# Cross attention on one Trainium2 core: six fold pairs in one piece ahead of the last batch's mixing, against two pieces of two inside it

## The chip, the core and the metric

The kernel runs on one core of one Trainium2 chip. The core has five engines with a queue each: TensorE (PE), VectorE (DVE), ScalarE (ACT), GpSimd (POOL) and SyncE (SP), which here issues most of the transfers. They meet only through semaphores. The metric is the device time of one execution in microseconds; lower is better.

## The reference, cut to what matters

The block is a Perceiver layer over 64 batches of 32 tokens of width 512, with 257 context rows each: cross attention, a small attention over heads, and a gated MLP. The change touches the cross attention alone:

```
xn = layernorm(x, ln_gamma, ln_beta)
q = (xn @ w_q).reshape(B, SQ, 16, 64)
k, v = split(context @ w_kv)            # 257 rows per batch
scores = einsum('bqhd,bkhd->bhqk', q * SCALE, k)
attn = softmax(scores)
out = einsum('bhqk,bkhd->bqhd', attn, v).reshape(B, SQ, 1024)
out = out @ w_out + b_out
```

The kernel never forms k or v. It folds the weight into the query, q·(w_k for that head), which gives a vector of width 512 for each head and token, takes scores of that against the raw context, mixes the raw context with the probabilities, and multiplies the mix by w_v.

## The kernel before

**Tiling.** `cross_attention` works in 16 turns (`TURNS`) of 4 batches (`GB`): 15 iterations of a hardware loop, `turn(t, True)`, and a last `turn(15, False)`. A turn has 128 tokens. Values that must keep their precision are kept as a high and a low part, and a product is three matmuls (`three`, L82 to L84).

**Folding.** `fold_pair(t, 1, j)` (L540) makes the folded queries of heads 2j and 2j+1 of the *next* turn: 8 matmuls, each of which is two records in the profile. A head has 64 elements, so its matmuls contract 64 rows, and two of them run side by side in the two halves of the array. Each pair fills two PSUM banks, one for each head. `FOLD_BANK` gives pairs 0, 3 the banks `A`, pairs 1, 4, 7 the banks `B2`, and pairs 2, 5, 6 the banks `C`, which are the banks that the transposed probabilities (`T_BANK`) use too. ScalarE copies each bank to a rounded high part (`high_fold`, L780), VectorE then subtracts that from the bank to get the low part (`low_fold`, L686), and raises `fold_lo`. `FOLD_AFTER` says how many of these low parts must be done before a later pair may overwrite the banks:

```
FOLD_BANK = (A, B2, C, A, B2, C, C, B2)
FOLD_AFTER = {3: 2, 4: 4, 5: 6, 6: 12, 7: 10}
```

So pair 3 waits for both low parts of pair 0, pair 4 for those of pair 1, pair 5 for those of pair 2.

**Mixing.** `mix_chunk(t, b, c)` makes a quarter of batch b's mix with six 512-column matmuls in bank 6 or 7, in turn. Before it starts it waits until the chunk two before it has been copied out by VectorE's `keep_mix` (L679): chunk 2 of batch 3 waits for `keep_mix(t, 3, 0)`, chunk 3 for `keep_mix(t, 3, 1)`. Chunk 0 also waits for the low parts of the batch's transposed probabilities (`pT_lo`). Between `keep_mix(t, 3, 0)` and the next copy VectorE has `keep_last` (a transpose, L691, a wait for it, and a multiplication, L694).

**Output.** `out_half(t, 0)` (L600 and L607) multiplies the mix by w_v; its products of chunk 3 wait for `keep_mix(t, 3, 3)`. Then come fold pairs 6 and 7, the first scores of the next turn and `out_half(t, 1)`.

**Order.** Every engine's order is written out by hand in its own `turn`. ScalarE's queue has the twelve high parts of pairs 0 to 5 in a row, and it is not edited.

Of the kernel before, what the change touches and what calls it, by code (L numbers as in the profile page):

```python
# [74 lines left out]
def f32(ap):  # L75

    return ap.bitcast(F32)
# [245 lines left out]
def cross_attention(nc, hw, ahead, ctx_nat, ctx_T, last_T, q_dram, v_dram, o_hi, o_lo, identity, heads):  # L323
# [9 lines left out]
    GB = P // SQ  # L333
    TURNS = B // GB
    KT = SK // P
# [5 lines left out]
    with ExitStack() as ctx:  # L341
# [34 lines left out]
        pT_hi, pT_lo = s.count("pT_hi", GB * KT), s.count("pT_lo", GB * KT)  # L376
# [20 lines left out]
        def of_head(a, h):  # L397

            return a[:, :, :, h * SQ:(h + 1) * SQ].rearrange("p c b n -> p (c b) n")
# [131 lines left out]
        def _(pe):  # L531
            def fold_pair(t, ahead, j):
                if j == 0:
                    pe.wait_ge(q_loaded.sem, q_loaded.at(t, 16 * (ahead + 1)))
                if j in FOLD_AFTER:
                    pe.wait_ge(fold_lo.sem, fold_lo.at(t, 2 * PAIRS * ahead + FOLD_AFTER[j]))
                for c in range(DC):
                    for h in range(2):
                        r = slice(h * HE, (h + 1) * HE)
                        mm = pe.matmul(ps[:, FOLD_BANK[j][h], c * P:(c + 1) * P], wk[r, j, c * P:(c + 1) * P],  # L540
                                       q[r, j, :], start=True, stop=True)
                mm.then_inc(fold_ready.sem, 1)
# [21 lines left out]
            def scores(t, b):  # L564
                pe.wait_ge(Tlo_done.sem, Tlo_done.at(t, b + 1))
                for i in range(TILES):
                    pe.wait_ge(exp_done.sem, exp_done.at(t, (b - 1) * TILES + i + 1))
                    score_tile(b, i)

            def turn_probs(t, b):  # L570
                for i in range(TILES):
                    pe.wait_ge(probs_ready.sem, probs_ready.at(t, b * TILES + i + 1))
                    for k in range(KT):
                        mm = pe.transpose(ps[:, T_BANK[k], i * P:(i + 1) * P], prob[:, i, k * P:(k + 1) * P], ident[:, :])
                        if i == TILES - 1:
                            mm.then_inc(turned.sem, 1)
# [34 lines left out]
            def turn(t, more):  # L611
                for b in range(GB - 1):
                    turn_probs(t, b)
                    scores(t, b + 1)
                    if b < GB - 2:
                        for c in range(DC):
                            mix_chunk(t, b, c)
                mix_chunk(t, 2, 0)
                mix_chunk(t, 2, 1)
                turn_probs(t, 3)  # L620
                mix_chunk(t, 2, 2)
                mix_chunk(t, 2, 3)
                if more:
                    fold_pair(t, 1, 0)
                    fold_pair(t, 1, 1)
                for c in range(DC):
                    mix_chunk(t, 3, c)
                    if more and c % 2 == 0:
                        fold_pair(t, 1, 2 + c)
                        fold_pair(t, 1, 3 + c)  # L630
                out_half(t, 0)
                if more:
                    fold_pair(t, 1, 6)
                    fold_pair(t, 1, 7)
                    for i in range(TILES):
                        first_scores(t, 1, i)
                out_half(t, 1)
# [15 lines left out]
        @block.vector  # L653
        def _(dve):
            def row_max(t, b, i):
                dve.wait_ge(scores_ready.sem, scores_ready.at(t, b * TILES + i + 1))
                dve.tensor_reduce(negmax[:, i:i + 1], ps[:, S_BANK[i], 0:SK], AX_X, ALU.max, negate=True)\  # L657
                    .then_inc(max_done.sem, 1)

            def invert(t, b, i):  # L660
                dve.wait_ge(exp_done.sem, exp_done.at(t, b * TILES + i + 1))
                dve.reciprocal(share[:, i:i + 1], total[:, i:i + 1]).then_inc(share_done.sem, 1)  # L662

            def softmax(t, b):
                for i in range(TILES):
                    row_max(t, b, i)
                    if i > 0:
                        invert(t, b, i - 1)
                invert(t, b, TILES - 1)

            def split_probs(t, b):
                for k in range(KT):
                    dve.wait_ge(pT_hi.sem, pT_hi.at(t, b * KT + k + 1))
                    dve.tensor_tensor(pT[b % 2][1][:, k, :], ps[:, T_BANK[k], :], f32(pT[b % 2][0][:, k, :]), ALU.subtract)\
                        .then_inc(pT_lo.sem, 1)

            def keep_mix(t, b, c):
                dve.wait_ge(mixed.sem, mixed.at(t, b * DC + c + 1))
                dve.tensor_copy(mix[:, c, b, :], ps[:, M_BANK[c % 2], :]).then_inc(mix_kept.sem, 1)  # L679

            def low_fold(t, ahead, j):
                for h in range(2):
                    n = 2 * j + h
                    dve.wait_ge(fold_hi.sem, fold_hi.at(t, 2 * PAIRS * ahead + n + 1))
                    hi, lo = (of_head(a, n) for a in fold)
                    dve.tensor_tensor(lo, ps[:, FOLD_BANK[j][h], :].rearrange("p (c n) -> p c n", n=SQ), f32(hi),  # L686
                                      ALU.subtract).then_inc(fold_lo.sem, 1)

            def keep_last(t):
                dve.wait_ge(last_ready.sem, last_ready.at(t, GB))  # L690
                dve.transpose(last_t[:, :, :], last_z[:, :, :]).then_inc(last_turned.sem, 1)  # L691
                dve.wait_ge(last_turned.sem, last_turned.at(t, 1))
                dve.wait_ge(o_ready.sem, o_ready.at(t, 0))
                dve.tensor_tensor(last_p[:, :, :, :],  # L694
                                  last_t[:, :, :].rearrange("p i (b q) -> p i b q", b=1).to_broadcast([P, TILES, GB, SQ]),
                                  own[:, :].rearrange("p (i b q) -> p i b q", i=1, q=1).to_broadcast([P, TILES, GB, SQ]),
                                  ALU.mult).then_inc(last_kept.sem, 1)

            def low_out(t, m):
                dve.wait_ge(o_hi_done.sem, o_hi_done.at(t, m + 1))  # L700
                dve.tensor_tensor(o[1][:, :, :], ps[:, O_BANK[m], :].rearrange("p (j n) -> p j n", n=P),
                                  f32(o[0][:, :, :]), ALU.subtract).then_inc(o_lo_done.sem, 1)

            def turn(t, more):
                for b in range(GB - 1):
                    split_probs(t, b)
                    softmax(t, b + 1)
                    if b < GB - 2:
                        for c in range(DC):
                            keep_mix(t, b, c)  # L710
                keep_mix(t, 2, 0)
                keep_mix(t, 2, 1)
                split_probs(t, 3)
                keep_mix(t, 2, 2)
                if more:
                    low_fold(t, 1, 0)
                keep_mix(t, 2, 3)
                if more:
                    low_fold(t, 1, 1)
                for c in range(DC):  # L720
                    keep_mix(t, 3, c)
                    if c == 0:
                        keep_last(t)
                    if more and c > 0:
                        low_fold(t, 1, 1 + c)
                    elif not more:
                        w_low(dve, range(2 * c + 1, 2 * c + 3, 2))
                if more:
                    low_fold(t, 1, 5)
                low_out(t, 0)  # L730
                if more:
                    low_fold(t, 1, 6)
                    low_fold(t, 1, 7)
                    softmax(t, GB)
                else:
                    w_low(dve, range(9, 15, 2))
                low_out(t, 1)
                if not more:
                    w_low(dve, range(15, PIECES, 2))

            dve.sem_inc(o_lo_done.sem, 2)
            dve.wait_ge(once, 16 + 16 * HT)
            for j in range(PAIRS):
                low_fold(0, 0, j)
            softmax(0, 0)
            dve.wait_ge(v_stored, 16)
            with dve.Fori(0, TURNS - 1) as t:
                turn(t, True)
            turn(TURNS - 1, False)

        @block.scalar
# [902 lines left out]
```

## Time and profile before

| | |
|---|---|
| median of 3 executions | 1916.24 us (1915.59 to 1916.68) |
| profiled execution | 1916.39 us, of which the span from first to last instruction is 1914.6 us |
| TensorE busy in the span | 1857.1 us (97%) |
| VectorE, ScalarE, GpSimd busy | 1039.1, 666.2 and 558.6 us |
| turn of the loop (islands of the same kind, 389.27 to 456.07) | 66.80 us |

A busy share is of the whole span. A matmul's row begins before the one ahead of it has ended, since the engine pipelines them; so the distance from start to start says what one costs. Times in the timeline views are from the start of the span. The idle time in brackets behind a row is that of the engine just before it, with what ended it. A row that stands for many instructions (x32) gives the start of the first and the time from there to the end of the last.

### The profile page before, as it was taken

How to read it: one execution, taken by the hardware profiler on the slowest of the kernel's cores; microseconds unless marked ns; L12 is line 12 of the kernel's file. 1: busy time of each engine (PE TensorE's matmuls, PEld its weight loads, DVE VectorE, ACT ScalarE, POOL GpSimd, SP SyncE). 2: the span in 40 equal slices, each digit the busy share in tenths (PEclk: the TensorE clock that was granted, in tenths of full speed). 3: DMA queues.
4: the chain of work that ended last, by engine and by line, in shares of the span. 5: the costliest groups of instructions: out<-in, count | busy, mean ns of one | idle time of the engine just before them, and what ended most of it. 6: DMA issues, size and time to landing. Idle time of an engine off the chain costs nothing. (4 is left out here: it accounts for less than half of the span.)

```text
span 1914.6 us, 36622 instructions
## 1 busy us (share of the span) xinstructions
PE 1857.1 (97%) x14096; PEld 1607.2 (84%) x14096; DVE 1039.1 (54%) x2015; ACT 666.2 (35%) x1356; POOL 558.6 (29%) x546
## 2 busy tenths in 40 slices
PE   5989999999999999999999999599999999999999
PEld 4868988988998898899989888488888788888887
DVE  7614555455455545545554555388889763333322
ACT  3235444444444444444444445221111231111111
POOL 3015334433533444353344436231112000000000
PEclk9999999999999999999999999799999999999999
DMA  7323223322322332232233223633352131000000
GB/s 244 128 85 99 86 61 103 99 77 77 110 78 66 99 99 78 76 110 77 67 98 99 81 73 127 184 84 88 99 154 73 57 126 65 3 34 32 21 24 22
DMA packets 166629, 165.65 MB, mean 87 GB/s; under 512 B 8688, under 2 KB 123888, under 8 KB 166576
## 3 DMA queue, kind: packets, MB, share of 16 engines
q1 hardware_dynamic: 162144, 156.27, 27.1%
q10 hardware_dynamic: 4432, 8.65, 1.2%
q8 instruction: 36, 0.59, 0.1%
q14 instruction: 17, 0.14, 0.0%
HBM read 131.08 MB, written 33.82 MB: 86 GB/s over the span
## 5 line engine op out<-in xcount | busy, mean ns | idle before, releaser
L497 POOL TENSOR_TENSOR x_prob<-x_prob,x_share 128x256 f32<-128x256 f32 x256 | 157.0, 613 | 602.9 <-DVE x_share L662 595.7
L82 PE MATMUL x_ps<-w_cT_hi,w_space_hi 128*128 128x258 f32 x1024 | 296.1, 289 | 0.0
L83 PE MATMUL x_ps<-w_cT_lo,w_space_hi 128*128 128x258 f32 x1024 | 290.7, 284 | 0.0
L84 PE MATMUL x_ps<-w_cT_hi,w_space_lo 128*128 128x258 f32 x1024 | 288.5, 282 | 0.0
L679 DVE COPY x_mix<-x_ps 128x512 f32<-128x512 f32 x256 | 176.2, 688 | 115.1 <-PE x_ps L84 114.9
L82 PE MATMUL x_ps<-x_pT_hi,x_cn_hi 128*128 128x512 f32 x512 | 208.1, 406 | 1.5 <-DVE x_mix L679 1.5
L686 DVE TENSOR_TENSOR w_space_lo<-x_ps,w_space_hi 128x512 fp32r<-128x512 f32 x256 | 161.0, 680 | 78.4 <-ACT w_space_hi L780 45.8
L84 PE MATMUL x_ps<-x_pT_hi,x_cn_lo 128*128 128x512 f32 x512 | 201.2, 393 | 0.0
L769 ACT ACTIVATE x_prob<-x_ps,x_negmax 128x257 f32<-128x257 f32 x256 | 122.1, 477 | 227.1 <-DVE x_negmax L657 227.1
L83 PE MATMUL x_ps<-x_pT_lo,x_cn_hi 128*128 128x512 f32 x512 | 199.7, 390 | 0.0
L657 DVE TENSOR_REDUCE x_negmax<-x_ps 128x1 f32<-128x257 f32 x256 | 108.1, 422 | 166.2 <-PE x_ps L84 166.2
L82 PEld LDWEIGHTS x_ps<-w_cT_hi,w_space_hi 128*128 128x128 f32 x1024 | 193.8, 189 | 2.0 <-issue 0.2
L83 PEld LDWEIGHTS x_ps<-w_cT_lo,w_space_hi 128*128 128x128 f32 x1024 | 193.8, 189 | 0.0
L84 PEld LDWEIGHTS x_ps<-w_cT_hi,w_space_lo 128*128 128x128 f32 x1024 | 193.5, 189 | 0.0
L780 ACT ACTIVATE w_space_hi<-x_ps 128x512 fp32r<-128x512 f32 x256 | 132.4, 604 | 124.0 <-PE x_ps L540 124.0
L491 POOL TENSOR_TENSOR x_cn_lo<-e_raw_n,x_cn_hi 128x1024 fp32r<-128x1024 f32 x64 | 153.3, 2395 | 0.0
L540 PEld LDWEIGHTS x_ps<-e_q,e_wk 64*128 64x128 f32 x2048 | 122.2, 192 | 27.7 <-issue 18.7
L486 POOL TENSOR_TENSOR w_cT_lo<-e_raw_T,w_cT_hi 128x1028 fp32r<-128x1028 f32 x64 | 141.5, 2210 | 5.8 <-ACT w_cT_hi L757 5.8
L540 PE MATMUL x_ps<-e_q,e_wk 64*128 64x128 f32 x2048 | 134.4, 282 | 7.5 <-SPq L465 4.9
L600 PE MATMUL x_ps<-x_mix,e_wv 128*64 128x128 f32 x2048 | 138.3, 275 | 0.8 <-DVE x_mix L679 0.8
L600 PEld LDWEIGHTS x_ps<-x_mix,e_wv 128*64 128x64 f32 x2048 | 114.2, 137 | 12.3 <-issue 5.4
L82 PEld LDWEIGHTS x_ps<-x_pT_hi,x_cn_hi 128*128 128x128 f32 x512 | 96.1, 188 | 23.6 <-DVE x_mix L679 1.9
(205 smaller groups left out, 3546.6 us busy)
## 6 DMA issues: line engine op xcount, KB each, us to landing
e_raw_T<-ctx_T SPq DMA_DIRECT2D x64, 514.0 KB, 4.0
e_raw_n<-ctx_nat SPq DMA_DIRECT2D x64, 512.0 KB, 3.6
q<-q_q ACTq DMA_DIRECT2D x16, 512.0 KB, 2.8
e_q<-q SPq DMA_DIRECT2D x16, 512.0 KB, 4.2
o_hi<-x_o_hi SPq DMA_DIRECT2D x32, 256.0 KB, 2.4
o_lo<-x_o_lo SPq DMA_DIRECT2D x32, 256.0 KB, 3.0
a_oT_hi<-o_hi SPq DMA_DIRECT2D x16, 512.0 KB, 4.4
a_oT_lo<-o_lo SPq DMA_DIRECT2D x16, 512.0 KB, 5.6
```

The source lines that it names most:

```text
L82: pe.matmul(out, lhs[0], rhs[0], start=start, stop=False)
L83: pe.matmul(out, lhs[0], rhs[1], start=False, stop=False)
L84: return pe.matmul(out, lhs[1], rhs[0], start=False, stop=stop)
L486: pool.tensor_tensor(cT[b % 2][1][:, :, 0:SK], raw_T[:, :, :], f32(cT[b % 2][0][:, :, 0:SK]), ALU.subtract).then_inc(Tlo_done.sem, 1)
L491: pool.tensor_tensor(cn[b % 2][1][:, :, :], raw_n[:, :, :], f32(cn[b % 2][0][:, :, :]), ALU.subtract).then_inc(nlo_done.sem, 1)
L497: pool.tensor_tensor(prob[:, i, 0:KT * P], prob[:, i, 0:KT * P], share[:, i:i + 1].to_broadcast([P, KT * P]), ALU.mult)\
L540: mm = pe.matmul(ps[:, FOLD_BANK[j][h], c * P:(c + 1) * P], wk[r, j, c * P:(c + 1) * P], q[r, j, :], start=True, stop=True)
L600: pe.matmul(out[h], w_v[:, c, n * HE:(n + 1) * HE], mix[:, c, :, n * SQ:(n + 1) * SQ], start=c == 0, stop=False)
L679: dve.tensor_copy(mix[:, c, b, :], ps[:, M_BANK[c % 2], :]).then_inc(mix_kept.sem, 1)
L686: dve.tensor_tensor(lo, ps[:, FOLD_BANK[j][h], :].rearrange("p (c n) -> p c n", n=SQ), f32(hi), ALU.subtract).then_inc(fold_lo.sem, 1)
L769: act.activation(prob[:, i, 0:SK], ps[:, S_BANK[i], 0:SK], ACT.Exp, bias=negmax[:, i:i + 1], accum_out=total[:, i:i + 1]).then_inc(exp_don ...
L780: act.activation(of_head(fold[0], 2 * j + h), ps[:, FOLD_BANK[j][h], :].rearrange("p (c n) -> p c n", n=SQ), ACT.Copy)\
```

## The change

On TensorE pairs 2, 3, 4 and 5 move from behind chunks 0 and 2 of batch 3's mixing to a place ahead of chunk 0, straight behind pairs 0 and 1. The wait for `pT_lo` that chunk 0 made is made ahead of pair 2, since its banks are those of the transposed probabilities. On VectorE all twelve low parts of pairs 0 to 5 stand in a row behind `keep_mix(t, 2, 3)`, ahead of the four copies of batch 3. The last turn, which folds nothing, keeps its order.

```
@@ tensor: turn
                 if more:
                     fold_pair(t, 1, 0)
                     fold_pair(t, 1, 1)
+                    pe.wait_ge(pT_lo.sem, pT_lo.at(t, GB * KT))
+                    for j in range(2, 6):
+                        fold_pair(t, 1, j)
                 for c in range(DC):
                     mix_chunk(t, 3, c)
-                    if more and c % 2 == 0:
-                        fold_pair(t, 1, 2 + c)
-                        fold_pair(t, 1, 3 + c)
                 out_half(t, 0)
@@ vector: turn
                 keep_mix(t, 2, 2)
-                if more:
-                    low_fold(t, 1, 0)
                 keep_mix(t, 2, 3)
                 if more:
-                    low_fold(t, 1, 1)
+                    for j in range(6):
+                        low_fold(t, 1, j)
                 for c in range(DC):
                     keep_mix(t, 3, c)
                     if c == 0:
                         keep_last(t)
-                    if more and c > 0:
-                        low_fold(t, 1, 1 + c)
-                    elif not more:
+                    if not more:
                         w_low(dve, range(2 * c + 1, 2 * c + 3, 2))
-                if more:
-                    low_fold(t, 1, 5)
                 low_out(t, 0)
```

TensorE's queue of before, from the last matmul of batch 2's mixing on. `e_q,e_wk` are the folds (x16 is two pairs), `x_pT,x_cn` the mixing, and a REGISTER_ALU row computes the value of a wait that stands there:

```order
L84 MATMUL x_ps<-x_pT_hi,x_cn_lo 128x512
L534 REGISTER_ALU
L540 MATMUL x_ps<-e_q,e_wk 128x128 x16
L587 REGISTER_ALU
L82 MATMUL x_ps<-x_pT_hi,x_cn_hi 128x512
L83 MATMUL x_ps<-x_pT_lo,x_cn_hi 128x512
L84 MATMUL x_ps<-x_pT_hi,x_cn_lo 128x512
L587 REGISTER_ALU
L82 MATMUL x_ps<-x_pT_hi,x_cn_hi 128x512
L83 MATMUL x_ps<-x_pT_lo,x_cn_hi 128x512
L84 MATMUL x_ps<-x_pT_hi,x_cn_lo 128x512
L540 MATMUL x_ps<-e_q,e_wk 128x128 x8
```

The same place of TensorE's queue in the changed kernel, up to the first matmul of chunk 0:

```order
L540 MATMUL x_ps<-e_q,e_wk 128x128 x16
L626 REGISTER_ALU
L540 MATMUL x_ps<-e_q,e_wk 128x128 x8
L536 REGISTER_ALU
L540 MATMUL x_ps<-e_q,e_wk 128x128 x8
L536 REGISTER_ALU
L540 MATMUL x_ps<-e_q,e_wk 128x128 x8
L536 REGISTER_ALU
L540 MATMUL x_ps<-e_q,e_wk 128x128 x8
L587 REGISTER_ALU
L82 MATMUL x_ps<-x_pT_hi,x_cn_hi 128x512
```

The six matmuls of chunk 0 that stood between pairs 1 and 2, and chunks 1 and 2 that stood between pairs 3 and 4, are behind all six pairs now; the waits on `fold_lo` (L536) of pairs 3, 4 and 5 have nothing but folds ahead of them.

VectorE's queue of before, from the copy of batch 2's chunk 2 on (`w_space_lo` is a low part of a fold, `x_mix` a copy of a mixing chunk):

```order
L679 COPY x_mix<-x_ps 128x512
L684 REGISTER_ALU
L686 TENSOR_TENSOR w_space_lo<-x_ps,w_space_hi 128x16x32
L684 REGISTER_ALU
L686 TENSOR_TENSOR w_space_lo<-x_ps,w_space_hi 128x16x32
L679 COPY x_mix<-x_ps 128x512
L684 REGISTER_ALU
L686 TENSOR_TENSOR w_space_lo<-x_ps,w_space_hi 128x16x32
L684 REGISTER_ALU
L686 TENSOR_TENSOR w_space_lo<-x_ps,w_space_hi 128x16x32
L679 COPY x_mix<-x_ps 128x512
L690 ISA
```

VectorE's queue of the changed kernel, from the last two of the twelve low parts on:

```order
L686 TENSOR_TENSOR w_space_lo<-x_ps,w_space_hi 128x16x32
L684 REGISTER_ALU
L686 TENSOR_TENSOR w_space_lo<-x_ps,w_space_hi 128x16x32
L679 COPY x_mix<-x_ps 128x512
L690 ISA
L691 STREAM_TRANSPOSE x_last_t<-x_last_z 128x128
L692 REGISTER_ALU
L693 ISA
L694 TENSOR_TENSOR x_last_p<-x_last_t,x_own 128x512
L679 COPY x_mix<-x_ps 128x512 x3
```

The copy of batch 3's chunk 0, which had four low parts ahead of it, has twelve ahead of it now, and the other three copies follow `keep_last` with nothing between them.

## Rows read from the trace of the kernel before

**Rows 1.** The page: busy time by engine, and the granted TensorE clock by slice

```profile
PE 1857.1 (97%) x14096; PEld 1607.2 (84%) x14096; DVE 1039.1 (54%) x2015; ACT 666.2 (35%) x1356; POOL 558.6 (29%) x546
PEclk9999999999999999999999999799999999999999
```

**Rows 2.** Busy time by stretch: wake of a long wait, the stage, a turn

```profile
core 0: us, PE busy (x) PEld busy (x) DVE busy (x) ACT busy (x) POOL busy (x), PEclk, DMA share, GB/s
140.00:144.00 4.00, 3.69 (x33) 3.47 (x34) 1.46 (x3) 1.21 (x3) 0.00 (x0) 0.58 0.02 4
389.27:401.37 12.10, 12.10 (x121) 9.86 (x120) 8.26 (x14) 6.20 (x12) 0.32 (x1) 1.00 0.25 81
389.27:456.07 66.80, 66.80 (x609) 60.28 (x608) 35.80 (x76) 30.48 (x66) 28.60 (x29) 1.00 0.29 87
```

**Rows 3.** The waits of TensorE between 200 and 1210 us

```profile
PE x_ps L82 <- DVE x_mix L679: 1.5, 1, 1.5
PE x_ps L600 <- DVE x_mix L679: 0.8, 1, 0.8
```

**Rows 4.** Timeline of TensorE around pairs 0 and 1 (start, duration, instruction)

```profile
388.95 0.40 PE L84 MATMUL x_ps<-x_pT_hi,x_cn_lo 128*128 128x512 f32 x1
389.27 2.06 PE L540 MATMUL x_ps<-e_q,e_wk 64*128 64x128 f32 x32
391.26 0.50 PE L82 MATMUL x_ps<-x_pT_hi,x_cn_hi 128*128 128x512 f32 x1
391.60 0.39 PE L83 MATMUL x_ps<-x_pT_lo,x_cn_hi 128*128 128x512 f32 x1
391.83 0.40 PE L84 MATMUL x_ps<-x_pT_hi,x_cn_lo 128*128 128x512 f32 x1
```

**Rows 5.** Timeline of TensorE, window 134.6 to 135.1: a fold's first six records

```profile
134.74 0.60 PE L540 MATMUL x_ps<-e_q,e_wk 64*128 64x128 f32 x6
```

**Rows 6.** Timeline of VectorE, same turn as rows 4

```profile
387.13 1.29 DVE L674 TENSOR_TENSOR x_pT_lo<-x_ps,x_pT_hi 128x512 fp32r<-128x512 f32 x2 [0.70 <-ACT x_pT_hi L775]
391.11 1.29 DVE L686 TENSOR_TENSOR w_space_lo<-x_ps,w_space_hi 128x512 fp32r<-128x512 f32 x2 [2.09 <-ACT w_space_hi L780]
...
394.11 0.68 DVE L679 COPY x_mix<-x_ps 128x512 f32<-128x512 f32 x1
394.71 0.30 DVE L691 STREAM_TRANSPOSE x_last_t<-x_last_z 128x128 f32<-128x128 f32 x1
395.14 0.69 DVE L694 TENSOR_TENSOR x_last_p<-x_last_t,x_own 128x512 f32<-128x512 f32 x1
...
401.48 0.69 DVE L679 COPY x_mix<-x_ps 128x512 f32<-128x512 f32 x1 [1.27 <-PE x_ps L84]
```

**Rows 7.** Timeline of ScalarE, same turn: high parts of pairs 0 and 1

```profile
390.48 2.07 ACT L780 ACTIVATE w_space_hi<-x_ps 128x512 fp32r<-128x512 f32 x4 [2.89 <-PE x_ps L540]
```

**Rows 8.** Timeline of VectorE in the kernel's opening folds: six low parts in a row

```profile
136.58 3.68 DVE L686 TENSOR_TENSOR w_space_lo<-x_ps,w_space_hi 128x512 fp32r<-128x512 f32 x6 [2.24 <-ACT w_space_hi L780]
```

**Rows 9.** Timeline of TensorE in the opening folds: pairs 3 to 5, then 6 and 7

```profile
134.74 2.95 PE L540 MATMUL x_ps<-e_q,e_wk 64*128 64x128 f32 x48
140.31 3.52 PE L540 MATMUL x_ps<-e_q,e_wk 64*128 64x128 f32 x32 [2.62 <-DVE w_space_lo L686]
```

**Rows 10.** Timeline of VectorE in the last turn, around a copy that comes late

```profile
1194.06 0.88 DVE L694 TENSOR_TENSOR x_last_p<-x_last_t,x_own 128x512 f32<-128x512 f32 x1
1194.86 1.78 DVE L394 TENSOR_TENSOR w_cT_lo<-e_wk,w_cT_hi 128x512 fp32r<-128x512 f32 x1
1196.56 0.68 DVE L679 COPY x_mix<-x_ps 128x512 f32<-128x512 f32 x1
```

**Rows 11.** Timeline of TensorE at the same place

```profile
1195.43 0.39 PE L84 MATMUL x_ps<-x_pT_hi,x_cn_lo 128*128 128x512 f32 x1
1197.29 0.50 PE L82 MATMUL x_ps<-x_pT_hi,x_cn_hi 128*128 128x512 f32 x1 [1.47 <-DVE x_mix L679]
1197.64 0.39 PE L83 MATMUL x_ps<-x_pT_lo,x_cn_hi 128*128 128x512 f32 x1
```

**Rows 12.** Timeline of TensorE where the mixing ends and the output begins

```profile
401.05 0.39 PE L84 MATMUL x_ps<-x_pT_hi,x_cn_lo 128*128 128x512 f32 x1
401.37 1.29 PE L600 MATMUL x_ps<-x_mix,e_wv 128*64 128x128 f32 x16
```

## The prediction

> **What bounds the kernel now.** I read the page first. TensorE is busy for 97% of the span, at the full clock nearly throughout [rows 1]. Then the windows view: one turn of the loop takes 66.80 us and TensorE is busy in all of it, at full clock [rows 2]. Then TensorE's waits: between 200 and 1210 us there are two, of 1.5 and 0.8 us, both on a VectorE copy of the mix and both in the last turn, which folds nothing [rows 3]. So in the 15 turns of the loop no engine holds TensorE up in a way that this view counts, and the time of a turn is the time of TensorE's own queue. What the change can give must be a cheaper queue on TensorE. What it can cost is any new wait there. I then read TensorE, VectorE and ScalarE over one turn, the one whose pair 0 starts at 389.27. Other turns differ by hundredths.
>
> **What is removed: two changes of form.** Before, TensorE goes from full-height matmuls to half-height folds and back three times in this stretch; after, once. The price is in [rows 4]. From the last mixing matmul, 388.95, to the second one behind the folds, 391.60, pass 2.65 us. Of that 0.23 is the normal step of a mixing matmul (391.60 to 391.83), twice: 0.46. The folds run two by two, 16 steps for two pairs. What does one step cost? A record of a fold lasts 0.27 (two records that start together after the first), so the x32 row's last pair of records starts 2.06 − 0.27 = 1.79 behind its first, 15 steps, and in [rows 5] the third starts 0.60 − 0.27 = 0.33 behind, 2 steps. With a first step a and later ones b: a + b = 0.33, a + 14b = 1.79, so b = 0.112 and a = 0.215. Sixteen plain steps are 1.79 us. The rest, 2.65 − 0.46 − 1.79 = 0.40 us, is the price of going in and out once. Two are removed: **−0.80 us a turn**. The Trainium skill, TensorEngine Tiling, Key Properties, says that changing the tiling mode drains TensorE; by that rule alone the change is a gain, and the trace agrees with the drain. The same page's section PSUM Bottleneck says the contrary for this change: tiling speeds up TensorE but not the emptying of PSUM, which may become the bottleneck. Rows decide between the two as follows.
>
> **What is added: waits on VectorE's drain.** A pair costs TensorE 8 × 0.112 = 0.90 us. It costs VectorE two low parts. Their pace is in [rows 8]: six in a row take 3.68, and the last lasts 0.68, so they start 0.60 apart, 1.20 us for each pair. ScalarE's high parts start (2.07 − 0.60)/3 = 0.49 apart [rows 7], 0.98 for each pair. VectorE is the slowest of the three and sets the rhythm. Mixing stood between the folds before and gave it the time; now it doesn't.
>
> Now the turn step by step. TensorE starts pair 0 at 389.27, and without a wait would start pair 3 at 389.27 + 0.10 + 3 × 0.90 = 392.07. VectorE starts the first low part at 391.11 [rows 6]; nothing ahead of it is in its way then, since it has idled for 2.09 us, and the copy of batch 2's chunk 3, which now stands ahead, can start at about 389.4, when that matmul ends, and takes 0.68. The low parts of pair j then start at 391.11 + 1.20j and 0.60 later, and the second ends 0.68 after that. How soon does TensorE go on? In [rows 8, 9] VectorE ends at 140.26 and TensorE starts at 140.31; in [rows 10, 11] at 1197.24 and 1197.29: 0.05. And a restarted engine pays a first step that is longer: 0.10 for folds (0.215 against 0.112), and 0.11 for mixing (1197.29 to 1197.64 is 0.35, normal 0.23).
>
> - Pair 3 waits for pair 0: released at 391.11 + 0.60 + 0.68 + 0.05 = 392.44, late by 0.37, restart 0.10.
> - Pair 4 is ready at 392.44 + 1.00 = 393.44, released at 393.64: 0.20, restart 0.10.
> - Pair 5 is ready at 394.64, released at 394.84: 0.20, restart 0.10.
> - Chunk 0 of batch 3 starts at 394.84 + 1.00 + 0.10 = 395.94. It needs no late copy; chunk 1 starts 0.11 + 6 × 0.23 = 1.49 later, at 397.43, and chunk 2 would at 398.81.
> - VectorE's thirteenth instruction of the row is the copy of chunk 0: it starts at 391.11 + 12 × 0.60 = 398.31 and ends at 398.99. Chunk 2 starts at 399.04: late by 0.23, restart 0.11.
> - Behind that copy comes `keep_last`: its transpose 0.60 later, its multiplication 0.43 after the transpose [rows 6], the next copy 0.61 after that (an instruction starts 0.08 before the end of the one ahead; 1194.06 + 0.88 against 1194.86 in [rows 10]). The copy of chunk 1 starts at 398.31 + 0.60 + 0.43 + 0.61 = 399.95 and ends at 400.63. Chunk 3, ready at 399.04 + 1.49 = 400.53, starts at 400.68: 0.15, restart 0.11.
> - Its last matmul starts 0.11 + 5 × 0.23 = 1.26 later at 401.94, and the output 0.32 behind that (401.05 to 401.37 in [rows 12]) at 402.26. Before, it started at 401.37.
>
> That is **+0.89 us a turn**. Summed the other way: waits 0.37 + 0.20 + 0.20 + 0.23 + 0.15 = 1.15, restarts 3 × 0.10 + 2 × 0.11 = 0.52, less 0.80: 0.87. I take 0.88. What matters is that the end of this stretch is one chain on VectorE from 391.11 to 400.63, with little left to TensorE: as long as VectorE is fed, the waits at pairs 3 to 5 don't add to it.
>
> Is it fed? ScalarE begins a pair's high parts about when the fold ends, and the first low part can start when the first high part is done, 1.84 us after the start of a pair in [rows 4, 6] (389.27 to 391.11). For pair 3: 392.44 + 1.84 = 394.28 against VectorE's 394.71; pair 4: 395.48 against 395.91; pair 5: 396.68 against 397.11. Slack 0.43 at each, so yes.
>
> The other edits cost nothing. The wait for `pT_lo` ahead of pair 2 is met: VectorE ended that work at 387.13 + 1.29 = 388.42 [rows 6], and pair 2 starts at 391.17. Uncovered, it would stop TensorE until that end. The copy of chunk 3 before the output is a wait now as before: VectorE has idled 1.27 us when it starts at 401.48, just behind the last mixing matmul [rows 6, 12], and after the change it is again idle then, having only copies left. VectorE is free 2.4 us sooner behind that, but pairs 6 and 7, the first scores and the high parts of the output wait for TensorE or ScalarE, so nothing comes back. ScalarE's and GpSimd's queues and the transfers keep their order and move with TensorE.
>
> **The sum.** 15 turns × 0.88 = 13.2 us on the profiled execution's 1916.39 gives 1929.6. The median of the runs shown is 0.15 lower: I say **1929.4 us**, 0.7% slower.
>
> **Bounds.** VectorE's pace enters about 13 times; at 0.01 either way it is 0.13 us a turn, 2 us in all. The release of 0.05 and the restart at 0.10 come in at the last wait once each; the nearest rows for them span 0.05 to 0.11. A restart inside folds at full clock is not in the trace, but it drops out of the VectorE chain. So 1927 to 1932 for this case alone.
>
> **The rivals.** About 0.2% (3.8 us) is what a measurement of this kernel can tell from no change.
>
> *The drain keeps up (faster).* TensorE would go through six pairs with no wait, and only the two changes of form would count: 15 × −0.80 = −12 us, 1904. This is where the rule on the drain of TensorE alone would lead. It decides at a VectorE pace of 0.45 us for each low part (half of a pair's 0.90), with the first release at or before 392.07. [Rows 8] show 0.60 with ScalarE working beside it, and [rows 6] the first release 0.37 too late even then. Chance 6%, with everything between it and no change.
>
> *The debt stays in the folds.* If VectorE caught up before chunk 2 (its copies jumping in somewhere, or faster than their rows), only 0.77 + 0.30 − 0.80 = +0.27 us a turn remains: +4, 1920. Against it: 12 × 0.60 is simple counting, and [rows 10, 11] show a late copy stopping TensorE just here, by 1.47 us in the last turn. Chance 6%, of which some 4% fall within 0.2%.
>
> *The clock falls (far slower).* In the opening folds, TensorE waited 2.62 us, and the next two pairs took 3.52 us where they take 2.06 at full clock [rows 4, 9]; the granted clock there was 0.58, a mix of full speed and half of it, 1.2 GHz [rows 2]. Were each turn to lose it for a stretch like that, it would add about 1.5 us: 15 × (0.88 + 1.5) = 36, 1952. Against it: the longest single wait that I find is 0.37 us, and the wait of 1.47 us in [rows 11] was followed by normal steps of 0.23 to 0.35. It decides at a wait between 1.47 and 2.62 us. Chance 3%.
>
> **How the numbers follow.** The forecast case has 85%. Together: faster 0.05, same 0.05, slower 0.90. The range for 8 in 10 is the forecast's own, widened a little for a term that I have missed by 0.15 to 0.3 us a turn: 1925 to 1933; it leaves the three rivals out, 15% in all.
>
> **What would show it.** In the timeline of a turn: one TensorE row of folds broken by waits on `w_space_lo` of 0.2 to 0.4 us less what the profile's overlap hides (a record outlives its step by 0.16, so waits of 0.20 may hardly be listed as idle); TensorE waits on `x_mix` ahead of chunks 2 and 3; twelve low parts as one unbroken VectorE row of about 7.3 us (11 × 0.60 + 0.68) without idle time, then the copy, and a distance of 12.99 us from pair 0 to the output where it was 12.10. The loop's turn grows to 67.68 us. I am wrong if VectorE's row has gaps (ScalarE then sets the pace), if it runs faster than 0.60, or if the granted clock drops inside the loop.

## The result, and the profile after

| | before | after |
|---|---|---|
| median | 1916.46 us (1915.59 to 1919.39, 4 runs) | 1930.70 us (1930.66 to 1931.03, 4 runs) |
| ratio | | 1.0072, 95% interval 1.0055 to 1.0089 |
| span of the profiled execution | 1914.6 us | 1928.9 us |

The change makes the kernel 14.2 us slower. 1929.4 us was forecast.

The page has TensorE busy for the same share as in [rows 1]. The granted clock by slice differs in the third slice alone, which ends ahead of the loop:

```profile
span 1928.9 us, 36622 instructions
PE 1866.5 (97%) x14096; PEld 1609.5 (83%) x14096; DVE 1040.8 (54%) x2015; ACT 667.7 (35%) x1356; POOL 559.0 (29%) x546
PEclk9989999999999999999999999799999999999999
```

The busy time of TensorE has grown by 9.4 us with the same number of instructions. That isn't more work: a record that overlaps its neighbour less counts for more.

The windows view, for the stage from pair 0 to the output and for one turn (columns as in [rows 2]; the turn chosen is again the fourth):

```profile
392.47:405.46 12.99, 12.62 (x121) 9.94 (x121) 10.76 (x18) 6.31 (x12) 0.33 (x1) 1.00 0.24 75
392.47:460.22 67.75, 67.38 (x609) 60.43 (x609) 35.91 (x76) 30.58 (x66) 28.64 (x29) 1.00 0.29 86
```

The stage takes 12.99 us where [rows 2] had 12.10. TensorE's matmuls are idle for only 0.37 us of it by this view, and the clock is full. The fourth turn takes 67.75 us where 67.68 was forecast. Turns differ by up to 0.11 us here, and by 0.08 before, so one turn is a rough measure: from pair 0 of the first turn to that of the fifteenth the mean is 67.70 us, against 66.85 before.

TensorE's timeline at the folds, and behind it at chunks 1 to 3 of the mixing and the output:

```profile
392.15 0.40 PE L84 MATMUL x_ps<-x_pT_hi,x_cn_lo 128*128 128x512 f32 x1
392.47 2.95 PE L540 MATMUL x_ps<-e_q,e_wk 64*128 64x128 f32 x48
395.66 3.55 PE L540 MATMUL x_ps<-e_q,e_wk 64*128 64x128 f32 x48 [0.23 <-DVE w_space_lo L686]
399.14 0.50 PE L82 MATMUL x_ps<-x_pT_hi,x_cn_hi 128*128 128x512 f32 x1
...
401.77 0.39 PE L84 MATMUL x_ps<-x_pT_hi,x_cn_lo 128*128 128x512 f32 x1
402.23 0.51 PE L82 MATMUL x_ps<-x_pT_hi,x_cn_hi 128*128 128x512 f32 x1
...
403.50 0.40 PE L84 MATMUL x_ps<-x_pT_hi,x_cn_lo 128*128 128x512 f32 x1
403.87 0.50 PE L82 MATMUL x_ps<-x_pT_hi,x_cn_hi 128*128 128x512 f32 x1
...
405.46 0.55 PE L600 MATMUL x_ps<-x_mix,e_wv 128*64 128x128 f32 x6
```

Both rows of folds hold three pairs. The first takes 2.95 us, the second 3.55: the 0.60 us more are the waits and restarts of pairs 4 and 5, which no idle figure of these rows names. Only the wait ahead of pair 3 is listed, as 0.23 us; from the starts it is 395.66 − 392.47 − 0.10 − 24 × 0.112 = 0.40, and 0.37 was forecast. At chunks 2 and 3 the distance from the matmul ahead is 0.46 and 0.37 where 0.23 is normal, and again nothing stands in brackets. Waits shorter than a record's overlap have to be read from start-to-start distances, or from the weight loads, which the profile lists as an engine of their own (PEld). A weight load's record is shorter, and each of the five waits stands in brackets there:

```profile
395.65 0.97 PEld L540 LDWEIGHTS x_ps<-e_q,e_wk 64*128 64x128 f32 x16 [0.42 <-DVE w_space_lo L686]
396.85 0.97 PEld L540 LDWEIGHTS x_ps<-e_q,e_wk 64*128 64x128 f32 x16 [0.23 <-DVE w_space_lo L686]
398.04 0.97 PEld L540 LDWEIGHTS x_ps<-e_q,e_wk 64*128 64x128 f32 x16 [0.22 <-DVE w_space_lo L686]
...
402.23 0.19 PEld L82 LDWEIGHTS x_ps<-x_pT_hi,x_cn_hi 128*128 128x128 f32 x1 [0.50 <-DVE x_mix L679]
...
403.87 0.19 PEld L82 LDWEIGHTS x_ps<-x_pT_hi,x_cn_hi 128*128 128x128 f32 x1 [0.41 <-DVE x_mix L679]
```

VectorE's timeline over the same stage, with ScalarE's twelve high parts as the last row (line numbers move with an edit: the high parts are L780 before and L775 here):

```profile
392.58 0.69 DVE L679 COPY x_mix<-x_ps 128x512 f32<-128x512 f32 x1 [0.36 <-PE x_ps L84]
394.31 7.26 DVE L686 TENSOR_TENSOR w_space_lo<-x_ps,w_space_hi 128x512 fp32r<-128x512 f32 x12 [1.04 <-ACT w_space_hi L775]
401.50 0.68 DVE L679 COPY x_mix<-x_ps 128x512 f32<-128x512 f32 x1
402.10 0.30 DVE L691 STREAM_TRANSPOSE x_last_t<-x_last_z 128x128 f32<-128x128 f32 x1
402.53 0.69 DVE L694 TENSOR_TENSOR x_last_p<-x_last_t,x_own 128x512 f32<-128x512 f32 x1
403.14 1.49 DVE L679 COPY x_mix<-x_ps 128x512 f32<-128x512 f32 x2
405.57 0.69 DVE L679 COPY x_mix<-x_ps 128x512 f32<-128x512 f32 x1 [0.94 <-PE x_ps L84]
...
393.68 6.66 ACT L775 ACTIVATE w_space_hi<-x_ps 128x512 fp32r<-128x512 f32 x12 [2.89 <-PE x_ps L540]
```

From 394.31 to the copy of chunk 1 VectorE has no gap but the 0.13 us in which `keep_last` waits for its own transpose. The copy of chunk 0 ends at 401.50 + 0.68 = 402.18 and chunk 2 starts at 402.23; the copy of chunk 1 ends 0.05 ahead of chunk 3 likewise. The last row, the copy of chunk 3, ends 13.79 us behind pair 0; in [rows 4, 6] it ended 12.90 us behind.

TensorE's waits between 200 and 1210 us, against [rows 3], where the loop had none (the two of the last turn come later than 1210 now):

```profile
PE x_ps L540 <- DVE w_space_lo L686: 3.3, 14, 0.2
```

The same view of the weight loads has two on VectorE at L540 and L82 that the loop of before didn't have:

```profile
PEld x_ps L82 <- DVE x_mix L679: 13.0, 29, 0.5
PEld x_ps L540 <- DVE w_space_lo L686: 12.2, 42, 0.4
```

That is 25.2 us in 14 turns. The forecast's waits and restarts, before the 0.80 that the change saves, are 1.67 us a turn, 23.4 in 14 turns.

### The profile page after: what moved, and what is told of

The parts are those of the page before. It is cut to its first block and busy times, and to the rows that moved or that the text cites. A ratio compares the mean times of both kernels' runs of the same rounds, so it can differ in the third digit from the quotient of the medians.

```text
span 1928.9 us, 36622 instructions
## 1 busy us (share of the span) xinstructions
PE 1866.5 (97%) x14096; PEld 1609.5 (83%) x14096; DVE 1040.8 (54%) x2015; ACT 667.7 (35%) x1356; POOL 559.0 (29%) x546
## 5 line engine op out<-in xcount | busy, mean ns | idle before, releaser
L82 PE MATMUL x_ps<-w_cT_hi,w_space_hi 128*128 128x258 f32 x1024 | 296.1, 289 | 0.0
L82 PE MATMUL x_ps<-x_pT_hi,x_cn_hi 128*128 128x512 f32 x512 | 207.9, 406 | 2.4 <-DVE x_mix L679 1.5
L82 PEld LDWEIGHTS x_ps<-w_cT_hi,w_space_hi 128*128 128x128 f32 x1024 | 193.7, 189 | 2.0 <-issue 0.2
L686 DVE TENSOR_TENSOR w_space_lo<-x_ps,w_space_hi 128x512 fp32r<-128x512 f32 x256 | 156.3, 682 | 62.9 <-DMA x_own<-identity 32.4
L775 ACT ACTIVATE w_space_hi<-x_ps 128x512 fp32r<-128x512 f32 x256 | 134.0, 604 | 64.1 <-PE x_ps L540 58.7
L540 PE MATMUL x_ps<-e_q,e_wk 64*128 64x128 f32 x2048 | 138.7, 284 | 12.0 <-DVE w_space_lo L686 6.1
L540 PEld LDWEIGHTS x_ps<-e_q,e_wk 64*128 64x128 f32 x2048 | 123.6, 192 | 30.1 <-DVE w_space_lo L686 16.8
L82 PEld LDWEIGHTS x_ps<-x_pT_hi,x_cn_hi 128*128 128x128 f32 x512 | 96.1, 188 | 33.5 <-DVE x_mix L679 15.4
```

Of the source, the lines that this page charges most:

```text
L82: pe.matmul(out, lhs[0], rhs[0], start=start, stop=False)
L775: act.activation(of_head(fold[0], 2 * j + h), ps[:, FOLD_BANK[j][h], :].rearrange("p (c n) -> p c n", n=SQ), ACT.Copy)\
```

## The experiments

For each run I read one distance in its trace, in the fourth turn of the loop: from the start of pair 0 to the end of the copy of chunk 3 of batch 3. The output needs that copy before it can go on. Before: 12.90; after: 13.79. The mean turn is that of the 14 turns from the first pair 0 of the loop to the fifteenth, against 66.85 us before.

| run | pair 0 to output | pair 0 to end of last copy | against before, a turn | mean turn against before | ratio to before (95%) |
|---|---|---|---|---|---|
| after | 12.99 | 13.79 | +0.89 | +0.85 | 1.0072 (1.0055 to 1.0089) |
| e_last_later | 12.72 | 13.52 | +0.62 | +0.59 | 1.0051 (1.0034 to 1.0068) |
| e_copies_first | 12.53 | 13.17 | +0.27 | +0.25 | 1.0017 (1.0008 to 1.0027) |
| e_copies_all | 12.38 | 13.18 | +0.28 | +0.23 | 1.0021 (1.0012 to 1.0031) |
| e_four_pieces | 12.52 | 13.32 | +0.42 | +0.39 | 1.0029 (1.0020 to 1.0039) |
| e_two_of_three | 11.68 | 12.48 | −0.42 | −0.44 | 0.9953 (0.9937 to 0.9970) |
| e_half_after | 11.59 | 12.39 | −0.51 | −0.53 | 0.9971 (0.9959 to 0.9983) |
| e_half_before | 12.10 | 12.90 | 0.00 | −0.02 | 0.9999 (0.9990 to 1.0009) |

e_last_later, e_copies_first, e_four_pieces and e_two_of_three ran on one chip, where the kernel before had 1918.06 us (19 runs), e_copies_all and the two with halved low parts on another, where it had 1917.15 (22 runs). The expectations name totals that start from 1916.5, so a total is to be judged against the kernel before on its own chip, as the ratio does. For every run, fifteen times the fourth column lies within the interval of the ratio.

**Copies ahead of the last low parts (e_copies_first).** VectorE's order alone is changed, from the changed kernel:

```
                 if more:
-                    for j in range(6):
+                    for j in range(5):
                         low_fold(t, 1, j)
                 for c in range(DC):
                     keep_mix(t, 3, c)
                     ...
+                    if more and c == 1:
+                        low_fold(t, 1, 5)
```

> The changed kernel, with TensorE's queue as it is, but VectorE's order altered: low parts of pairs 0 to 4, the copies of batch 3's chunks 0 and 1, then the low parts of pair 5, then the copies of chunks 2 and 3. Theory (one chain on VectorE from the first low part to the copy of chunk 1): the copies are no longer late, the waits ahead of chunks 2 and 3 go (0.23 + 0.11 + 0.15 + 0.11 = 0.60 us a turn), those at pairs 3 to 5 stay; pair 0 to output 12.40 us where the changed kernel has 12.99; total 1921 to 1922 us. Rival (the loss is made at the waits of pairs 3 to 5, the copies don't matter): no change, 1930.7 us.

Measured: 1921.51 us. The time is inside what the theory gave, but partly because the kernel before was 1.6 us slower on this chip: against it the run is 3.5 us slower, where the theory had 4.5 to 5.5. The trace gives 15 × 0.27 = 4.1. The rival, that the copies don't matter, is out: the intervals of 1.0017 and 1.0072 lie apart. But pair 0 to output was 12.53 and not 12.40. VectorE's timeline shows why (pair 0 starts at 391.18 here), and TensorE's gives the output:

```profile
401.78 1.28 DVE L686 TENSOR_TENSOR w_space_lo<-x_ps,w_space_hi 128x512 fp32r<-128x512 f32 x2
402.98 1.37 DVE L679 COPY x_mix<-x_ps 128x512 f32<-128x512 f32 x2
```

```profile
403.71 0.76 PE L600 MATMUL x_ps<-x_mix,e_wv 128*64 128x128 f32 x9
```

The low parts of pair 5 stand ahead of the copy of chunk 2. It starts at 402.98 and, at 0.68, ends at 403.66, 0.05 ahead of the output. That was my order, not the change's.

**Last low parts behind all copies (e_copies_all).** From e_copies_first:

```
-                    if more and c == 1:
-                        low_fold(t, 1, 5)
+                if more:
+                    low_fold(t, 1, 5)
```

> The changed kernel, TensorE's queue as it is, VectorE's order: low parts of pairs 0 to 4, all four copies of batch 3, low parts of pair 5 last. The run with the copies of chunks 0 and 1 first gave 12.53 us from pair 0 to the output where 12.40 was expected; in its trace the low parts of pair 5 push the copy of chunk 2 back to 12.48, and the output starts 0.05 after it. Theory (that copy is what is missing): 12.40 us here, 15 x 0.13 = 2 us less than that run, 1.5 to 2.5 us. Rival (the 0.13 has another cause): 12.53 us again.

Measured: pair 0 to output 12.38 us, so the late copy was what was missing from that mark. The total was 1920.96, a ratio of 1.0021 against 1.0017 there: nothing was gained, where I had expected 1.5 to 2.5 us. The intervals of the two ratios are as wide as that, so it is the trace that decides. VectorE's timeline (pair 0 at 390.15):

```profile
402.64 0.69 DVE L679 COPY x_mix<-x_ps 128x512 f32<-128x512 f32 x1 [0.69 <-PE x_ps L84]
```

This last copy ends at 403.33, 13.18 behind pair 0. In e_copies_first the last copy ends at 402.98 + 1.37 = 404.35, 13.17 behind. The output's products of chunk 3 wait for it in either run. An output that starts 0.15 us sooner waits 0.15 us longer inside itself: its first 16 records take 1.12 us up to the next row in e_copies_all (the first two rows), and 0.96 in e_copies_first (the other two).

```profile
402.53 1.29 PE L600 MATMUL x_ps<-x_mix,e_wv 128*64 128x128 f32 x16
403.65 0.39 PE L607 MATMUL x_ps<-x_last_p,x_last_v 128*64 128x128 f32 x4
...
403.71 1.13 PE L600 MATMUL x_ps<-x_mix,e_wv 128*64 128x128 f32 x16
404.67 0.39 PE L607 MATMUL x_ps<-x_last_p,x_last_v 128*64 128x128 f32 x4
```

So the start of the output is the wrong mark, and the end of the last copy the right one; for the forecast of the change both give 0.89.

**The `keep_last` pair later (e_last_later).** From the changed kernel:

```
                     keep_mix(t, 3, c)
-                    if c == 0:
+                    if c == 1:
                         keep_last(t)
```

> The changed kernel, with the transpose and the multiplication of keep_last moved from behind the copy of chunk 0 to behind the copy of chunk 1. Theory (the chain on VectorE): the copy of chunk 1 comes 1.04 us sooner, and chunk 3 no longer waits; what goes is 0.14 of wait and 0.11 of restart, 0.25 us a turn: pair 0 to output 12.74 us, total 1927 us. Rival (the copies don't matter): no change, 1930.7 us.

Measured: 1928.15 us, and 13.52 us to the end of the last copy, 0.27 less than the changed kernel. The theory gave 0.25. Two instructions that nobody waits for at that moment cost 15 × 0.27 = 4 us by standing ahead of a copy that somebody does wait for. The ratios, 1.0051 and 1.0072, differ by as much, but their intervals overlap; against the rival speaks the trace.

**Two pieces of three (e_two_of_three).** From the kernel before (the wait for `pT_lo` ahead of pair 2 as in the change). Only TensorE's lines are shown; VectorE's low parts and copies are moved to the order that the expectation names:

```
+                    fold_pair(t, 1, 2)
                 for c in range(DC):
                     mix_chunk(t, 3, c)
-                    if more and c % 2 == 0:
-                        fold_pair(t, 1, 2 + c)
-                        fold_pair(t, 1, 3 + c)
+                    if more and c == 1:
+                        for j in range(3, 6):
+                            fold_pair(t, 1, j)
```

> The kernel before, with two pieces of three pairs in place of three of two: pairs 0 to 2, chunks 0 and 1 of batch 3, pairs 3 to 5, chunks 2 and 3; VectorE empties pairs 0 to 2, copies chunks 0 and 1, empties 3 and 4, copies chunks 2 and 3, empties 5. Theory (0.40 us for each going in and out of half-height folds; waits only where the drain is late): no wait is left, one change of form less, pair 0 to output 11.70 us where before has 12.10, total 15 x 0.40 = 6 us less, 1910.5 us. Rival (going in and out costs nothing of its own, the first and last step of a piece are only shown longer): 1916.5 us. Rival (any fold that has three ahead of it waits for the drain): above 1918 us.

Measured: 1910.0 us, ratio 0.9953, faster than both kernels. Against the kernel before on its chip that is 8.1 us less, where 6 were expected and the trace gives 15 × 0.42 = 6.3. TensorE's fold rows and the output, and the windows view of the stage:

```profile
389.96 2.95 PE L540 MATMUL x_ps<-e_q,e_wk 64*128 64x128 f32 x48
...
395.80 2.95 PE L540 MATMUL x_ps<-e_q,e_wk 64*128 64x128 f32 x48
401.64 1.29 PE L600 MATMUL x_ps<-x_mix,e_wv 128*64 128x128 f32 x16
```

```profile
389.96:401.64 11.68, 11.68 (x121) 9.86 (x120) 9.57 (x16) 6.10 (x12) 0.30 (x1) 1.00 0.26 79
```

Both pieces take 2.95 us, so there is no wait in either, and chunks 0 and 1 give VectorE its time between them. One going in and out less is 0.42 us a turn.

**Four pieces (e_four_pieces).** From the kernel before: pair 0, chunk 0, pairs 1 and 2, chunk 1, pair 3, chunk 2, pairs 4 and 5, chunk 3, and VectorE's low parts behind them in that order (only TensorE's lines are shown).

```
                     fold_pair(t, 1, 0)
-                    fold_pair(t, 1, 1)
                 for c in range(DC):
                     mix_chunk(t, 3, c)
-                    if more and c % 2 == 0:
-                        fold_pair(t, 1, 2 + c)
-                        fold_pair(t, 1, 3 + c)
+                    if more and c < 3:
+                        for j in ((1, 2), (3,), (4, 5))[c]:
+                            fold_pair(t, 1, j)
```

> The kernel before, with four pieces in place of three: pair 0, chunk 0, pairs 1 and 2, chunk 1, pair 3, chunk 2, pairs 4 and 5, chunk 3; VectorE's low parts follow in the order of the pairs. Theory: one more going in and out of half-height folds and no new wait, pair 0 to output 12.50 us, 15 x 0.40 = 6 us more, 1922.5 us. Rival (going in and out costs nothing): 1916.5 us.

Measured: 1923.45 us (ratio 1.0029), 5.4 us more than the kernel before on its chip where 6 were expected, and +0.42 us a turn in the trace. So one going in and out more costs what one less gives.

**Half the low parts (e_half_after, e_half_before).** Only the length of 16 VectorE instructions of a turn differs, in the changed kernel and in the one before:

```
+                    if ahead:
+                        hi, lo, src = (a[:, 0:DC * GB // 2, :] for a in (hi, lo, src))
```

> The changed kernel, in which the low parts of the folds inside the loop are made for half of the columns only (the other half keeps the values of the opening folds), so that the numbers are not those of the reference; only the length of 16 VectorE instructions a turn differs, no order and no wait. Theory (the loss is VectorE's pace): VectorE needs about 0.35 us for each where it needed 0.60, ScalarE's 0.49 becomes the slowest, and the six pairs meet waits of 0.1 us or less: pair 0 to output about 11.5 us where the changed kernel has 12.99, total some 8 us under before, about 1909 us. Rival (six pairs in one piece cost time in themselves, by restarts or by the longer reach to the output): above 1916.5 us still.

> The kernel before, with the same halved low parts inside the loop (again not the reference's numbers). Control: both theories say that VectorE is hidden there, pair 0 to output 12.10 us as in the full kernel, total 1916.5 us.

Measured: 1912.07 us (ratio 0.9971) for the one, 1917.18 (0.9999) for the other. With shorter low parts, the same order of six pairs in one piece is faster than three pieces of two; before the change the same shortening gives nothing. VectorE's and ScalarE's timelines of e_half_after (pair 0 at 388.68), and TensorE's fold row:

```profile
390.52 5.82 DVE L689 TENSOR_TENSOR w_space_lo<-x_ps,w_space_hi 128x256 fp32r<-128x256 f32 x12 [1.04 <-ACT w_space_hi L777]
```

```profile
389.89 6.00 ACT L777 ACTIVATE w_space_hi<-x_ps 128x512 fp32r<-128x512 f32 x12 [2.89 <-PE x_ps L540]
```

```profile
388.68 5.93 PE L540 MATMUL x_ps<-e_q,e_wk 64*128 64x128 f32 x96
```

A half low part takes 0.42 us, yet twelve of them start (5.82 − 0.42)/11 = 0.49 us apart. That is ScalarE's pace, (6.00 − 0.60)/11 = 0.49: ScalarE is now the slowest of the three. It is still a little too slow for TensorE, whose six pairs without waits would take 0.10 + 48 × 0.112 + 0.16 = 5.64 us and take 5.93. So the gain is 0.51 and not 0.80 a turn. Two things of the expectation were off: a half low part was to take 0.35 us, and pair 0 to output was to be about 11.5, where 11.59 was measured.

The total, 1912.07, is 3 us above the 1909 expected (executions went from 1906.77 to 1914.45). In the profiled one the turns took 66.33 us on average, 0.53 less than before, which is 7.9 us in 15. But its first pair 0 came 0.94 us later than before, and the part behind the attention took 2.4 us more, in code that the edit doesn't touch. There the mean granted clock was lower in two stretches: 0.88 against 0.92 around 1240 us, and 0.83 against 0.91 around 1490 us. What moved it is open.

## Why the prediction was right, step by step

- *TensorE's own queue sets the time of a turn.* Right: in e_half_before the low parts are shorter and the stage stays at 12.10 us.
- *−0.80 for two changes of form.* Right: 0.42 for one less, 0.42 for one more, against 0.40. With both gone, in e_half_after, the stage is 0.51 shorter with 0.29 of waits in it, which makes 0.80.
- *VectorE sets the rhythm at 0.60.* Right: (7.26 − 0.68)/11 = 0.60, no gap in the row of twelve.
- *Waits at pairs 3 to 5.* Right, with pair 3 at 3.19 us behind pair 0 against 3.17, and in sum: from pair 0 to chunk 0 pass 6.67 us in the changed kernel; 6.67 were forecast (395.94 − 389.27).
- *Late copies at chunks 2 and 3.* Right: chunk 2 starts 9.76 us behind pair 0 (9.77 forecast), chunk 3 11.40 (11.41), and 0.62 us a turn goes when the copies move up (13.79 to 13.17), against 0.60.
- *`keep_last` in the chain.* Right: 0.27 against 0.25.
- *+0.89 us a turn from pair 0 to output.* Measured 12.99 against 12.99.
- *Nothing comes back behind the output.* Nearly: the stage costs 0.89 and the mean turn 0.85, so 0.03 to 0.04 us come back somewhere in the rest of the turn. Where isn't shown.

The total was 1.3 us more than forecast, and the loop isn't where it came from. Pair 0 of the first turn and of the fifteenth start at

```profile
189.45 0.38 PE L540 MATMUL x_ps<-e_q,e_wk 64*128 64x128 f32 x2
...
1137.27 0.49 PE L540 MATMUL x_ps<-e_q,e_wk 64*128 64x128 f32 x4
```

against 188.82 and 1124.74 before: 14 turns have grown by 11.90 us, 0.85 each and not 0.88, so 15 turns give 12.8 us of the 14.3 by which the profiled executions differ. But 0.63 us had been lost ahead of the first turn, in code that the change doesn't touch. Of that, some lies in the opening folds:

```profile
123.44 5.00 PE L540 MATMUL x_ps<-e_q,e_wk 64*128 64x128 f32 x48 [4.91 <-SPq L465]
```

Before, the same 48 records took 4.58 us. The windows view from this row to the next has a lower granted clock after (second line) than before (first line), a mix of full speed and half of it in both:

```profile
123.22:127.73 4.51, 4.51 (x49) 4.39 (x49) 0.39 (x1) 2.06 (x3) 2.42 (x6) 0.62 0.24 51
123.44:128.38 4.94, 4.94 (x49) 4.82 (x49) 0.98 (x2) 2.06 (x3) 2.44 (x6) 0.56 0.27 54
```

In e_half_before, which in the end is as fast as before, the 48 records took 5.49 us. So this looks like a difference between executions at the kernel's start, where TensorE comes out of a wait of 4.91 us. Behind the attention the changed kernel loses about 1 us more. A wait for a transfer there is 16.1 us where it was 15.6. Most of the rest is lost in the 16 us behind that wait, where the mean granted clock is 0.72 and was 0.74; that the clock accounts for it is likely and not shown. No experiment was made on it. So the loop alone would have given about 1929 us. The 1.6 us outside it were in no forecast, and such differences can fall either way: the kernel before alone went from 1914.28 to 1919.15 us on one chip.

The rivals: the drain that keeps up was settled by e_half_after, which is what it would look like, and its turning point lies below 0.49 us, where 0.29 us of waits are left; 0.45 was forecast, and no run is there. The debt that stays in the folds is what e_copies_all is, made on purpose: +0.28 a turn against the +0.27 forecast. The falling clock did not come: it stayed at full level in the loop (1.00 in the windows above). By the Trainium skill, TensorEngine Tiling, Key Properties, changing the tiling mode drains the engine. The runs with one piece less and one piece more agree that each change has a price, 0.42 us a piece; that the price is a drain isn't something that they show. The Trainium skill, TensorEngine Tiling, PSUM Bottleneck, says that tiling speeds up TensorE but not the emptying of PSUM, and names a fourfold speedup as where the copies may become the bottleneck. Here it was reached with matmuls of half height, two at a time, as e_half_after shows.

## What to carry to other kernels

Grouping work that has its own form on TensorE pays for each change of form that it saves, but only up to the length that the engines behind it can empty: compare the pace of TensorE for one unit (0.90 us here) with that of the slowest engine that empties it (1.20), and cut the group where the first reuse of a bank would wait. Then look at what stands behind the group in the emptying engine's queue, since a debt made in the group is paid by the next reader of that queue; in this case moving that reader up gave 0.62 us of a loss of 0.89. When a mark moves and the total doesn't, look for a second wait behind the mark.

## What the runs showed of the hardware that was not expected

- A wait of 0.2 us with its restart costs TensorE 0.30 us here and shows up as no idle time ahead of a matmul, since a record of a fold lasts 0.27 us and its step 0.11. The waits view of the matmuls has 3.3 us in 14 turns, that of the weight loads 25.2, against some 23 us of waits and restarts.
- Going in and out of half-height matmuls costs 0.42 us each time (two runs, one with a piece less and one with a piece more), whether the piece has one, two or three pairs.
- VectorE's row of low parts kept its 0.60 us pace over twelve instructions (394.31 to 401.57) while ScalarE read other banks for most of that time (393.68 to 400.34) and TensorE wrote into others.
